# Two transformer layers on one core: loads, rows, splits of x and stores at other places, and a new table of places

## What is computed

```
for layer in (0, 1):
    xn = layernorm(x)                      # per row of 512
    x  = x + attention(xn) + mlp(xn)
attention: Q, K, V = xn @ W.T; 16 heads of 32; rotary on Q, K
           scores = Q K^T / sqrt(32), causal; softmax; @ V; @ Wo.T
mlp:       (silu(xn @ gate.T) * (xn @ up.T)) @ down.T
           hidden 2048 in layer 0, 1408 in layer 1 (with scales there)
```

## Time and profile before

| | us |
|---|---|
| median of the runs | 1997.6 |
| the profiled execution, its own time | 1996.87 |
| its span, first to last instruction | 1995.2 |
| TensorE busy | 1846.7 |
| ScalarE busy | 1091.1 |
| VectorE busy | 1067.9 |
| GpSimd busy | 720.2 |

### The profile page before, as it was taken

The page is one execution under the profiler, slowest core; times in us unless marked ns, Lnnn a source line. Parts: engine busy times, 40 slices in busy tenths (PEclk is TensorE's granted clock), DMA queues, the critical chain, the costliest instruction groups (busy, mean ns, idle before and its releaser), DMA issues.

```text
span 1995.2 us, 24662 instructions
## 1 busy us (share of the span) xinstructions
PE 1846.7 (93%) x8656; PEld 1350.9 (68%) x8656; DVE 1067.9 (54%) x2368; ACT 1091.1 (55%) x2445; POOL 720.2 (36%) x628
## 2 busy tenths in 40 slices
PE   5999999999998999999989989999998889999988
PEld 4777767676776576756467767777776755767564
DVE  5546556472545374737346474555536544646462
ACT  2565657574246484747426556565732554757572
POOL 4234343432433244424133252435334334343331
PEclk9999999999999899999889989999999989999999
DMA  6213121220131121203142031214112212121201
GB/s 221 54 43 90 44 80 44 74 82 23 62 80 49 43 73 52 82 20 114 64 132 75 23 101 43 69 44 122 43 32 69 74 33 80 44 80 38 64 12 42
DMA packets 66122, 130.32 MB, mean 65 GB/s; under 512 B 7504, under 2 KB 8528, under 8 KB 64976
## 3 DMA queue, kind: packets, MB, share of 16 engines
q1 hardware_dynamic: 66000, 128.75, 22.0%
HBM read 73.67 MB, written 4.19 MB: 39 GB/s over the span
## 4 chain that ended last, share of the span: by engine, by line
PE 72%; DVE 11%; ACT 7%; POOL 4%; issue 3%; DMA 2%; SPq 0%; DVEq 0%; POOLq 0%; ACTq 0%
PE D L940 17%; PE G L940 12%; PE U L940 10%; PE OE L1038 7%; PE OE L940 7%; PE SS L1022 6%; PE SS L940 5%; PE OE L1022 3%; PE OE L1001 3%; PE SS L1001 3%; DVE xres L909 2%; POOL wgl L715 2%; ACT OE L636 2%; DVE OE L867 1%; ACT pr L655 1%
## 5 line engine op out<-in xcount | busy, mean ns | idle before, releaser
L909 DVE TENSOR_TENSOR xres<-D,xres 128x512 f32<-128x512 f32 x352 | 238.6, 688 | 262.5 <-PE D L940 259.6
L655 ACT ACTIVATE pr<-SS 128x512 f32<-128x512 f32 (+3 forms) x512 | 233.7, 498 | 148.8 <-PE SS L1022 147.7
L747 POOL TENSOR_TENSOR hl<-tt,hh 128x512 fp32r<-128x512 f32 x108 | 139.2, 1289 | 376.7 <-ACT hh L673 376.3
L636 ACT ACTIVATE OE<-OE,mp 128x384 f32<-128x384 f32 (+3 forms) x256 | 203.9, 798 | 102.4 <-DVE mp L867 101.6
L867 DVE CUSTOM_DVE_ANT_0 OE<-OE,mask 128x384 f32<-128x384 f32 (+3 forms) x256 | 220.5, 873 | 59.1 <-PE OE L1001 57.5
L765 POOL TENSOR_SCALAR_AFFINE_SELECT pr<-pr 128x512 f32<-128x512 f32 x128 | 81.3, 638 | 379.7 <-ACT pr L655 379.6
L1022 PE MATMUL SS<-QS,KS 98*128 98x512 f32 (+2 forms) x512 | 178.0, 395 | 18.8 <-DMA QS<-mt 11.4
L940 PE MATMUL G<-xh,wgh 128*128 128x512 f32 x432 | 178.4, 413 | 16.0 <-DVE tt L920 8.5
L636 ACT ACTIVATE SS<-SS,mp 128x128 f32<-128x128 f32 (+3 forms) x256 | 162.1, 634 | 51.7 <-DVE mp L867 50.2
L867 DVE CUSTOM_DVE_ANT_0 SS<-SS,mask 128x128 f32<-128x128 f32 (+3 forms) x256 | 169.7, 676 | 32.8 <-PE SS L1001 32.3
L940 PE MATMUL D<-wdh,hh 128*128 128x512 f32 x432 | 174.8, 405 | 9.3 <-DVE xres L909 4.5
(11 more groups left out here) (123 smaller groups left out, 3760.8 us busy)
## 6 DMA issues: line engine op xcount, KB each, us to landing
KS<-pr SPq DMA_DIRECT2D x128, 192.0 KB, 3.3
QS<-pr SPq DMA_DIRECT2D x128, 192.0 KB, 3.3
raw<-in_wgate_dram SPq DMA_DIRECT2D x27, 512.0 KB, 3.6
raw<-in_wup_dram SPq DMA_DIRECT2D x27, 512.0 KB, 3.6
raw<-in_wdown_dram SPq DMA_DIRECT2D x27, 512.0 KB, 3.7
raw<-in_wqk_dram SPq DMA_DIRECT2D x16, 512.0 KB, 3.5
trig<-in_wv_dram SPq DMA_DIRECT2D x4, 1024.0 KB, 7.2
trig<-in_rope_dram SPq DMA_DIRECT2D x4, 1024.0 KB, 5.2
```

What stands on the lines that cost most here:

```text
L636: act.activation(s, s, ACT.Exp, bias=mp[:, c, at:at + 1], scale=-1.0, accum_out=se[:, c, at:at + 1]) \
L655: act.activation(weights(i)[:, h, skip:W], SB[(i * HG + h) % 3][:, skip:W], ACT.Exp, scale=-1.0) \
L747: pool.tensor_tensor(hl[:, fc, :], tt[:, (blk * nfc + fc) % 2, :], hh[:, fc, :].bitcast(F32), ALU.subtract) \
L909: dve.tensor_tensor(xres[:, rt, :], d[:, :], xres[:, rt, :], ALU.add).then_inc(sem["v_dfree"], 1)
```

## The change

- `loads` takes the load of the next weights out of the step `w` and puts it 8 steps later in the list (`BEHIND`), at the latest ahead of the next `w` of the same slot. It waits for the same split as before.
- `v_weights` goes from the third last item of a layer to the item of the last `pv`.
- `x_next` takes one chunk: chunk 0 behind set 7 of the last turn, chunk 1 behind the last `pv`. The rows of chunk 0 go one by one behind the four last `wo`, and the statistics and the first two normalised tiles behind the fourth; the item that held them is gone.
- `values` 4 goes ahead of the last transpose in `opening`.
- `store` writes one tile of 256 KB as soon as its last `down` is added: 16 stores in all instead of 4.
- The table `PACE` is new in all 16 rows; between 3 and 34 of about 100 digits of a row differ. Matmuls and vector work are the same in kind and number.

```diff
+BEHIND = 8
@@ plan
-    items += [[("pv", n - 2), ("pv", n - 1), ("heads", 1)] + [("x_next",)] * (l == 1 and not final)] + output(1)
+    items.append([("pv", n - 2), ("pv", n - 1), ("heads", 1)] + [("v_weights", 1 - l)] * (not final))
+    items += output(1)
+    if l == 1 and not final:
+        halves = [k for k, it in enumerate(items) if ("pv", TPC * 2 - 1) in it]
+        items[halves[-1]].append(("x_next", 0))
+        items[-TPC - 1].append(("x_next", 1))
+        for rt in range(TPC):
+            items[rt - TPC].append(("row", 0, rt))
+        items[-1] += normal(0)
...
-        items[-3].append(("v_weights", 1))
     else:
-        d0[-1].append(("store", 0))
-        d1[-1].append(("store", 1))
+        for c, d in enumerate((d0, d1)):
+            for i, piece in enumerate(d):
+                piece.append(("store", c * TPC + i))
...
-            items += [[("row", 0, rt) for rt in range(TPC)] + normal(0)] + norms(0, range(TPC))
-            items[-3].append(("v_weights", 0))
+            items += norms(0, range(TPC))
...
+def loads(steps):
+    out, due = [], []
+    for x in steps:
+        while due and (due[0][0] <= len(out) or x[0] == "w" and SLOT[x[1]] in [SLOT[kind] for _, kind in due]):
+            out.append(("load", due.pop(0)[1]))
+        out.append(x)
+        if x[0] == "w":
+            due.append((len(out) + BEHIND, x[1]))
+    return out + [("load", kind) for _, kind in due]
...
@@ opening
-    ... later[2] + later[3] + [("keep", 1)] * (layer == 0) + [values[4]]
+    ... later[2] + [values[4]] + later[3] + [("keep", 1)] * (layer == 0)
@@ PACE: batch 0 layer 0, turns 0 and 3; batch 0 layer 1, turn 3; batch 1 layer 1, turn 3
-        ("01020030100011001113020311130203111010111002000000110010000101110000000010010000010010000011000000000",
+        ("01300020100100011012030202111212021020010010020000110101000101000001000010100000010010000011000000000",
-         "002000110101100120130302021112120210200100100200001300100001010000010000100100000100100000112010w030"),
+         "00100020101100111013030202111212021020010012000000110101000101000001000010100000010010000011811q0211"),
-         "00100020001011100022020311221121110000000000000000000000000000000000000000000000000000000000101026000"),
+         "0010002001001200010220321212110001000000000000000000000000000000000000000000000000000000000010107020"),
-         "03000210102000201020212121212111000000000000000000000000000000000000000000000000000000000001010"),
+         "0000021010200020100203212121100010000000000000000000000000000000000000000000000000000000000d000"),
@@ SyncE
-            def w(n, kind):
+            def load_next(n, kind):
                 follows = n.follows(SLOT[kind])
                 if follows:
-                    sp.wait_ge(sem["g_lo"], n("g_lo", 1))
+                    sp.wait_ge(sem["g_lo"], n.ready(kind))
                     load(sp, *follows, raw[:, SLOT[kind], :], f"raw{SLOT[kind]}")
-            def store(n, c):
+            def store(n, rt):
                 sp.wait_ge(sem["v_dfree"], n("v_dfree"))
-                sp.dma_start(rows(out, n, c, n.b), xres[:, c * TPC:(c + 1) * TPC, :]).then_inc(sem["d_out"], 16)
+                sp.dma_start(out[n.b, rt * P:(rt + 1) * P, :], xres[:, rt, :]).then_inc(sem["d_out"], 16)
```

More of the change, by code:

```diff
@@ L54 @@
 RING = 4
-TILES = True
+BEHIND = 8
+SLOT = {"A": 2, "O": 2, "U": 0, "G": 1, "D": 1}
+SLOTS = 3
 DIGITS = "0123456789abcdefghijklmnopqrstuvwxyzABCDEFGHIJKLMNOPQRSTUVWXYZ"
@@ L236, in layer @@
     first, items, pieces = plan(b, l)
-    return first + paced(items, pieces, PACE[b][l])
+    return loads(first + paced(items, pieces, PACE[b][l]))
+def loads(steps):
[7 more added lines that the diff above has]
+    return out + [("load", kind) for _, kind in due]
 def opening(layer):
@@ L246, in opening @@
     out += [("stats", layer, 1), ("xn", layer, TPC), ("xn", layer, TPC + 1), proj[0], values[0], values[1], ("rotate", 0)]
-    out += values[2:4] + later[0] + [proj[1]] + later[1] + later[2] + later[3] + [("keep", 1)] * (layer == 0) + [values[4]]
+    out += values[2:4] + later[0] + [proj[1]] + later[1] + later[2] + [values[4]] + later[3] + [("keep", 1)] * (layer == 0)
     return out + [*values[5:], ("rotate", 1), proj[2], ("rotate", 2), proj[3], ("rotate", 3)]
@@ new lines @@
+        ("41000010100100102053201302031113021020010110100000000000000000000000000000000000000000000000000000030",
+         "00000021000101010113031112111112121030011001000000100010000100200001000010000000000000000000000000003",
+         "00000201010101010113031203020212121020110100100000110010000101000000000000000000000000000000000000000",
+         "0010002001001200010220321212110001000000000000000000000000000000000000000000000000000000000010107020"),
+    ),
+    (
+        ("30000030101001001113020311121203111010111002100100100000000101110000000010010000010010000011000000000",
+         "00100020100021001212000411121121111020010110100000110010002100100000000010010000010020101000000000101",
+         "11001030000100010113031213021121212011101001000000100010000101000001000010100000001002100010000000002",
+         "00200011010110012013030202111212021020010010200000110101000101000001000010100000010010000011820p0010"),
+        ("30000030101010102103005111211112121010100010001000100010010100100000000000000000000000000000000000000",
+         "01000220011000101014020312111112121030011001000000100010000100200001000000000000000000000000000000004",
+         "00000201010101010113031203020212121020110100100001000010000100000000000000000000000000000000000000003",
+         "0000021010200020100203212121100010000000000000000000000000000000000000000000000000000000000d000"),
@@ L285 @@
     "keep": {},
-    "x_next": {"d_x0": 16, "d_x1": 16},
+    "x_next": {},
+    "load": {},
     "xn": {"v_xn": 1},
@@ L314 @@
 STACKS = 16
-SLOT = {"A": 2, "O": 2, "U": 0, "G": 1, "D": 1}
-SLOTS = 3
 SPLITS_OPEN = "ADGU"
@@ L361, in follows @@
     def follows(self, slot):
-        later = SPLITS[slot][self.taken[slot] + 1:]
+        later = SPLITS[slot][self.taken[slot]:]
         return later[0][:2] if later else None
@@ L385, in did @@
         if step[0] == "x_next":
-            self.batches += 1
+            self.batches += step[1] == 0
+            self.n[f"d_x{step[1]}"] += 16
         if step[0] in ("add_wo", "add_down"):
@@ L571, in keep, with x_next @@
                 sp.dma_start(xres[:, c * TPC:(c + 1) * TPC, :], rows(x, n, c, n.batches)).then_inc(sem[f"d_keep{c}"], 16)
-            def x_next(n):
+            def x_next(n, c):
                 sp.wait_ge(sem["p_pv"], n("p_pv"))
[L575 to L578, removed]
+                sp.dma_start(val[:, c * TPC:(c + 1) * TPC, :], rows(x, n, c, n.b + 1)).then_inc(sem[f"d_x{c}"], 16)
             def rotate(n, t):
@@ L595, in flip @@
                                  mt[k * HG * TPC:(k + 1) * HG * TPC, c, :].bitcast(F32)).then_inc(sem["d_shift"], 16)
-            def w(n, kind):
+            def load_next(n, kind):
                 follows = n.follows(SLOT[kind])
                 if follows:
-                    sp.wait_ge(sem["g_lo"], n("g_lo", 1))
+                    sp.wait_ge(sem["g_lo"], n.ready(kind))
                     load(sp, *follows, raw[:, SLOT[kind], :], f"raw{SLOT[kind]}")
-            def store(n, c):
+            def store(n, rt):
                 sp.wait_ge(sem["v_dfree"], n("v_dfree"))
-                sp.dma_start(rows(out, n, c, n.b), xres[:, c * TPC:(c + 1) * TPC, :]).then_inc(sem["d_out"], 16)
-            walk(dict(v_load=v_load, v_weights=v_weights, keep=keep, x_next=x_next, rotate=rotate, flip=flip, w=w, store=store))
-            sp.wait_ge(sem["d_out"], CREDIT["d_out"] + 16 * NC * B)
+                sp.dma_start(out[n.b, rt * P:(rt + 1) * P, :], xres[:, rt, :]).then_inc(sem["d_out"], 16)
+            walk(dict(v_load=v_load, v_weights=v_weights, keep=keep, x_next=x_next, rotate=rotate, flip=flip, load=load_next, store=store))
+            sp.wait_ge(sem["d_out"], CREDIT["d_out"] + 16 * RT * B)
         @block.scalar
```

14 lines of the change are left out of this document (2 added, 12 removed).

## The result

The changed kernel takes 1924.68 us, the median of four runs (1924.21 to 1929.51), against 1996.35 of the kernel before in its own four. The ratio is 0.9649, with a 95% interval of 0.9628 to 0.967: 3.5%, or 70 us. The profiled execution took 1924.21 us.

The account below looks back on a forecast made before the run. TensorE was taken as the bound, busy 1846.7 of 1995.2 us, plus gaps, with 136 us at 1.2 GHz. A to F 36.6, G 3 and H 3 sum to 42.6: 1955 us median, range 1932 to 1984, chance 0.62.

Parts of the forecast that it names:

- A: Four openings: values 4 covers the fourth transpose's wait for a normalised tile; gain 9.0 us, bounds 0 and 9.
- B: Behind flip, layer 1 turn 0, both batches: later load removes two stalls on small DMAs; 11.2 us, bounds 7.3 and 11.4.
- C: Between the batches: pieces and earlier x fill three gaps; 5.8 us after charges, bounds 2 and 7.6.
- D: Between layers 0 and 1, twice: wo pieces and earlier V splits shorten waits; about 6.0 us, bounds 2 and 9.
- E: At the end: pieces and four last wo fill the last down's wait for GpSimd; 2.6 us, bounds 0 and 2.9.
- F: Last store: a 256 KB transfer lands sooner than 1 MB; gain 2.0 us, bounds 0 and 2.
- G: Rest of the new table, nat steps and turn starts: gaps mostly move elsewhere; gain 3 us, bounds -8 and 20.
- H: Clock: fewer 1.2 GHz stretches behind removed waits; gain 3 us, bounds -15 and 14.
- Half of it comes back: Rival: gaps are filled but the next nat or st waits instead; about 20 us gain, 1978 us, chance 0.25.
- The clock eats it: Rival: time at the low clock doubles, 136 us more, costing 34 to 68; about 1997 us, no change, chance 0.07.
- The loads come late: Rival: delayed loads miss their splits and hold up ScalarE; 1.2 us late each gives 2020 us, slower, chance 0.06.

Follow-up runs that it names:

- experiment 1: The changed kernel with the old PACE table put back, so only the new steps: 1969.79 us, ratio 0.9854 to the kernel before.
- experiment 6: The changed kernel with V weights, next x, row statistics and first normalised tiles back at their old places, new digits kept: 1935.81 us, ratio 0.968.
- experiment 10: The kernel before with only the digits of the last items of each last turn new: 1989.19 us, ratio 0.9975.
- experiment 2: The kernel before, old steps kept, with the new table (one digit 0 added for the item still there): 1967.81 us, ratio 0.9846.
- experiment 3: The kernel before with only the weight loads 8 steps later: 1977.57 us, ratio 0.9893.
- experiment 4: The kernel before with only values 4 moved ahead of the last transpose: 1983.5 us, ratio 0.9929.
- experiment 8: The changed kernel with rows of its own table, chosen as faster in the trace, used in both batches: 1916.34 us, ratio 0.959.
- experiment 12: The changed kernel with values 4 back behind the last transpose: 1943.26 us, ratio 0.973.
- experiment 5: The changed kernel with the weight loads back in their step w: 1947.83 us, ratio 0.9746.
- experiment 7: The kernel before with only stores by tile and ten pieces ahead of the last four wo: 1995.65 us, ratio 0.9983.
- experiment 9: The kernel of experiment 8 with the old digits up to the last pv in layer 1's last turn and chunk 0's stores together: 1918.0 us, ratio 0.9605.
- experiment 11: The kernel of experiment 8 with seven instead of six pieces ahead of nat 4 in each layer's first turn: 1918.47 us, ratio 0.9604.

## Why the prediction was right and wrong

**A to F, right.** They summed to 36.6, and the trace shows:

| step | predicted | measured in gaps |
|---|---|---|
| A, `values` 4 | 9.0 | 9.0: four waits of 2.26, 2.26, 2.24, 2.26 gone |
| B, loads | 11.2 | 11.3: no `QS<-mt` wait left |
| C, between batches | 5.8 | 5.3: of 7.9 us (1.92, 4.22, 0.30, 1.45), 2.6 are left (0.77, 1.78) |
| D, between layers, twice | 6.0 | 6.6 |
| E, end | 2.6 | 2.7: 2.91 became 0.17 |
| F, last store | 2.0 | 2.3: 5.5 behind the last matmul became 3.2 |

Two steps hold only with an addition. C counted on seven pieces between the statistics and the transpose; experiments 1 and 6 say that the new digits did more for the 4.22 us than the moved rows (3.55 left with the rows moved alone, nothing with the digits alone). D's first tile of layer 1 still waits (1.57 in batch 0, 2.47 in batch 1, against 2.25), as worked out.

**G, right in gaps, wrong in time.** It was put at 3, and the gaps outside A to F did fall by 3.4 (38.5 + 2.3 - 0.2, less the 37.2 of the table). But the table alone gained 31 us, which is more than its upper bound of 20. A part of that belongs to the boundaries, where experiment 10 put the ends of the rows alone and gained 5. The rest, some 26 us, is within the turns: the profile of experiment 2 has only 3.5 us less of gaps than that of experiment 10, but 16.6 us less of busy time and 25.6 us less at 1.2 GHz. That is the misjudged sentence of G: a piece taken from one place "leaves a hole in another". Holes were moved; which of them are followed by the low level changed. Why these digits are better at that is not shown.

**H, the step that failed.** "If all the low stretches behind the waits of A to E went [...] 14. But gaps of the table fall and rise without regard to this. I take 3, bounds -15 and 14." Measured: the time at 1.2 GHz fell from 136 to 71 us, and busy time by 32.2, ten times the term and more than twice its upper bound. Some 48 us of low stretches went behind the waits of A to E (27 behind the two of B, 7 each at A, C and E), as named; the rest, about 17, went within the turns. Two things were undersized. First, the price: taking the busy time of the first ten profiles of this study against their time at the low level gives 0.49 us of busy time per us, near to the half that the prediction gave for a TensorE that never waits, where I had charged some 0.25 for the longest stretches. Second, the rest, which I put at nothing or less. Of its 17 us, 10 are the stretch in the last turn of batch 0 (20.5 us before; 3.4 and 6.8 after), and that one is no sure gain of the change: it was 6.8 us in experiments 3 and 4, which leave TensorE's steps there alone, and 17.1 in experiments 6 and 8, whose digits there are the ones of the kernel after.

How much of the 32.2 us of busy time is the clock's own can be worked out in three ways, all of them estimates. The slope over ten profiles gives 0.49 x 65.5 = 32. Within the low stretches TensorE was busy 120.6 us before and 67.5 after; half of the difference is 26.6. By a third reading the clock is worth less: over the runs of one kernel a mean clock higher by 0.001 goes with 1.1 us less, which for 0.016 is 17 us; that a slower TensorE also waits less behind such a stretch would explain it, and is not shown. So the clock's share lies between 17 and 32.

Range and terms did not fit each other either: the upper bounds of A to H add up to 75.9 us, which is 1922, below the 1932 that I gave as the end.

**A removed wait was worth more than its length here.** This is what the experiments add, and what takes the place of H as a separate term. Gap and time in us, with what the time is known to:

| part | gap | time | known to | ratio of the two |
|---|---|---|---|---|
| A alone (4) and undone (12) | 9.0 | 14, 16 | 6, 6 | 1.6, 1.8 |
| B alone (3) | 11.3 | 21 | 4.5 | 1.9 |
| loads undone (5) | 16.6 | 19 | 7 | 1.2 |
| C and D undone (6) | 5.0 | 6 | 7 | 1.2 |
| E and F alone (7) | 5.0 | 3.4 | 3 | 0.7 |
| the whole change | 40.6 | 70 | 4 | 1.7 |

A ratio above 1 is clear of noise for B alone and for the whole change, and barely for undoing A; the others can't be told from 1. F is no gap of TensorE at all, and behind E only some 15 us are left in which the clock could matter. With 1.7 for the 39.6 of A to G the forecast would have been 67 us, 1930; but 1.7 is taken from this very result, so that is no test of it.

**The rivals.** "Half of it comes back" did not come: TensorE's waits for ScalarE in `nat` fell by 3 us, and the gaps in `st` other than the two behind `flip` rose by 2 only (11.9 to 13.8). "The clock eats it" has the right actor and the wrong sign. "The loads come late" did not come: no split of gate, up or down waits for `raw` in the trace, and experiment 3, which delays every load on the old table, is 21 us faster.

**The two rules.** The Trainium skill ("TensorE: Matmul & The Clock Gate", section "Part 1: The HAM clock gate") says that the throttled state is the default and activity lifts it. The trace agrees at the long waits: all ten behind `flip` of 5.4 to 5.8 us, in the profiles of six kernels, reach into a low stretch of 6.8 to 13.7 us. It does not explain 20.5 us at the low level with TensorE busy for 20.35 of them. The page's advice is against long gaps, but it also tells of a kernel that swings between the two levels because TensorE idles briefly and often between groups of matmuls, and I made nothing of that; here waits of 2.21 to 2.26 us were followed by the low level 14 times of 24. I also read the Trainium skill's rule on batching transfers ("DMA: Bandwidth & Descriptors", section "Bandwidth") as making F a loss. The rule is on bandwidth, and here only the landing of the last store is waited for: the 256 KB stores landed in 2.1 us against 5.3 for 1 MB, and the end is 2.3 us shorter.

**Left open.** Why the same gaps are followed by 6.8 us at the low level in one kernel and by 20.5 in another (below) was not settled; nor whether a table chosen with the clock in mind would beat experiment 8. Experiments 9 and 11, each aimed at one place, gained nothing: the gap came up again elsewhere.

## What to carry to other kernels

Where TensorE is over 90% busy and the mean granted clock is below 1, don't count a closed gap at its length alone: look in the windows around it for a stretch at the low level, and add up to half of it, knowing that in another kernel the same wait may have none. Compare TensorE's busy time at equal instruction counts first; if it moved, look at the clock: over ten profiles here it moved by 0.49 us for each us at the low level. And a table of places and the steps that it places are one thing: each alone gave 29 and 31 us, together 70, and digits for one boundary opened a wait of 4.6 to 5.9 us at the other.

## What the runs showed of the hardware

- A wait of TensorE of 2.21 to 2.26 us in product code was followed by 3.4 us at 1.2 GHz four times out of four in experiment 12, twice of four in the kernel before, and 14 times of 24 over six profiles. Waits behind `flip` of 5.4 to 5.8 us reached into 6.8 to 13.7 us of it ten times out of ten.
- The same code behind the same gaps has stretches of different length from kernel to kernel, all at 0.50: the `st` of the last turn of batch 0 were low for 20.5 us in the kernel before and in experiment 7, for 6.8 in experiments 1, 3 and 4. This stretch of the kernel before had hardly a gap inside it:

```profile
946.20:966.70 20.50, 20.35 (x75) 0.50 0.01 1
```

- A kernel's own runs spread with its clock: experiment 4 ran from 1972.52 us at 0.976 to 1991.13 at 0.963, some 1.5 us for each 0.001, without any change of the program.
- Small DMAs in SP's queue cost what stands ahead of them: with the load in front and SP waiting for the split, there were two waits of 5.81 and 5.64 us behind `flip`; without them, and with a low stretch elsewhere that was shorter, the kernel was 21 us faster (experiment 3). With `flip` first, only a weight load waited 0.28 us for its second 8 KB DMA.
